# Summing passes of a four-layer graph network: key numbers read from PSUM, and twelve gather buffers in place of six

## The reference

```python
edge_index = jnp.stack([src, dst])
x = x + L0(h, edge_attr)          # sum of edge features by dst, then an MLP
x = x + L1(h, edge_attr)          # attention over the edges of a node
# L2: sums in both directions
agg_fwd = segment_sum(w[:, None] * x[col], row)
agg_bwd = segment_sum(w[:, None] * x[row], col)
out = 0.5 * (agg_fwd @ W_src.T + b_src) + 0.5 * (agg_bwd @ W_dst.T + b_dst)
# L3: weighted mean over src rows by dst, matmul, layernorm
ssum = segment_sum(edge_weight[:, None] * node[src], dst)
```

## Time and profile before

| | us |
|---|---|
| median of 3 runs | 9346.08 (9331.73 to 9353.26) |
| the profiled execution: its own time | 9342.07 |
| the profiled execution: span from first to last instruction | 9340.4 |
| forward L2 pass, first gather to last addition | 5389.4 to 6194.1 |
| backward L2 pass | 6896.4 to 7573.4 |
| L3 pass | 8432.1 to 9140.3 |
| mean granted TensorE clock | 0.881 |

### The profile page before, as it was taken

One profiled execution on the slowest core, in us unless ns is written; L12 is line 12 of the kernel. 1 busy time (PEld: TensorE's weight loads), 2 busy tenths in 40 slices (PEclk: granted clock), 3 DMA queues, 4 the chain that ended last, 5 costly groups with the idle time before them and its releaser, 6 DMA issues. The chain is left out here.

```text
span 9340.4 us, 229910 instructions
## 1 busy us (share of the span) xinstructions
PE 7261.6 (78%) x60542; PEld 5838.2 (63%) x60851; DVE 6413.4 (69%) x20871; ACT 3252.4 (35%) x9379; POOL 4037.3 (43%) x4385
## 2 busy tenths in 40 slices
PE   4855677899968888888868977758877775886777
PEld 4855566544446666666667766646666664666665
DVE  5999888511167777777777766656666676666667
ACT  3533322222223333333235500025520025557882
POOL 2000577000057777777625567730037740006771
PEclk7975789999977777777789999989999988999997
DMA  0000466300024444444347866665556644556663
GB/s 21 2 2 1 110 140 140 91 24 24 23 73 105 107 105 106 106 105 105 91 147 271 289 183 191 191 156 230 230 199 191 192 156 178 230 230 183 184 182 106
DMA packets 645062, 1262.07 MB, mean 135 GB/s; under 512 B 126526, under 2 KB 183433, under 8 KB 644569
## 3 DMA queue, kind: packets, MB, share of 16 engines
q1 hardware_dynamic: 424337, 704.50, 23.0%
q0 software_dynamic: 199040, 544.46, 21.7%
q10 hardware_dynamic: 21452, 10.20, 0.4%
HBM read 780.96 MB, written 477.75 MB: 135 GB/s over the span
## 5 line engine op out<-in xcount | busy, mean ns | idle before, releaser
L1063 PE MATMUL PS<-w,GS 128*128 128x128 f32 x12176 | 1641.7, 284 | 499.9 <-DVE AREA L1008 224.2
L1063 PEld LDWEIGHTS PS<-w,GS 128*128 128x128 f32 x12176 | 1459.6, 192 | 682.3 <-DVE w L967 437.6
L1188 POOL DMA_INDIRECT GS<-xbuf,KI x964 | 1031.2, 1070 | 1759.7 <-ACTq L132 710.1
L1171 POOL DMA_INDIRECT GS<-t1d,KI x1564 | 1493.6, 955 | 488.0 <-issue 459.6
L2395 DVE TENSOR_SCALAR AREA<-PS,IP 128x512 bf16<-128x512 f32 x1116 | 837.7, 751 | 439.6 <-PE PS L2405 361.1
L967 DVE TENSOR_TENSOR w<-IO,KI 128x512 f32<-128x512 f32 (+1 forms) x1355 | 808.6, 597 | 424.6 <-issue 413.4
L2419 PE MATMUL PS<-AREA 128*128 x13392 | 961.1, 220 | 11.1 <-ACT GS L2373 1.4
L2419 PEld LDWEIGHTS PS<-AREA 128*128 128x128 bf16 x13392 | 843.8, 98 | 170.2 <-issue 49.2
L2373 ACT ACTIVATE GS<-PS 128x512 f32<-128x512 f32 x1116 | 666.3, 597 | 613.8 <-PE PS L2419 613.5
L1188 POOL DMA_INDIRECT GS<-pbuf,XR x558 | 595.3, 1067 | 209.4 <-issue 101.4
L1598 ACT ACTIVATE w<-PS,w 128x48 f32<-128x48 f32 x1564 | 341.7, 301 | 926.9 <-PE PS L1593 926.9
(11 more groups left out here) (410 smaller groups left out, 12508.2 us busy)
## 6 DMA issues: line engine op xcount, KB each, us to landing
xbuf<-GS SPq DMA_DIRECT2D x1116, 256.0 KB
XR<-in_edge_attr SPq DMA_DIRECT2D x780, 256.0 KB
pbuf<-AREA SPq DMA_DIRECT2D x482, 256.0 KB
GS<-t1d,KI POOLq DMA_INDIRECT x1564
GS<-xbuf,KI POOLq DMA_INDIRECT x964
GS<-pbuf,XR POOLq DMA_INDIRECT x558
AREA<-t2d ACTq DMA_DIRECT2D x121, 64.0 KB
keyd<-AREA POOLq DMA_INDIRECT x482
```

Of the source, the lines that this page charges most:

```text
L1063: i = e.matmul(PS[:, s % 3, 0:128], feats(s)[0:m, r, 0:D], SELW[s % 3][0:m, width * r:width * r + 128], start=(r == 0), stop=(r == 3))
L1171: e.indirect_dma_start(GS[0:m, s, r, 0:wide], None, table, bass.IndirectOffsetOnAxis(ap=idx[0:m, c:c + 1].bitcast(U32), axis=0)).then_inc( ...
L1188: e.indirect_dma_start(GF[:, 512 * s:512 * s + 512], None, buf, bass.IndirectOffsetOnAxis(ap=idx[:, b:b + 1].bitcast(U32), axis=0)).then_i ...
```

## The change

Three edits, all in code that the three summing passes use:

- `sel` reads the numbers 0 to 127 from PSUM (bank 7, the first 128 columns), where one `tensor_copy` at the start of each pass puts them. The keys stay in SBUF. Layer 0 goes on reading `IO` from SBUF.
- Twelve gather buffers (`GRING`): six in `GS` as before, six in `R`, the last third of `AREA`. GpSimd waits for `bd` from the thirteenth batch on (`b - GRING + 3`).
- The loops of VectorE, TensorE and ScalarE in these passes unroll 12 batches (`un=GRING`) and go round half as often. The 12 bounds of 6 batches are still loaded with one load for each 6 batches, twice in a round now. 558 = 46 x 12 + 6 and 482 = 40 x 12 + 2, so 6 and 2 batches follow the loop, each with a load of its own (before: none and 2).

```diff
-    def batches(e, nb, step):
+    def batches(e, nb, step, un=UN):
...
-        n = nb // UN
+        n = nb // un
         with e.Fori(0, n) as it:
-            for s in range(UN):
-                step(it * UN + s, s, it, False)
+            for s in range(un):
+                step(it * un + s, s, it, False)
...
-    def unit_ranges(e, nb, part):
+    def unit_ranges(e, nb, part, un=UN):
...
-            if s == 0:
-                held[0] = ranges(e, part, it * (2 * UN), 2 * UN)
-            return held[0][2 * s:2 * s + 2]
+            if s % UN == 0:
+                held[0] = ranges(e, part, it * (2 * un) + 2 * s, 2 * UN)
+            return held[0][2 * (s % UN):2 * (s % UN) + 2]
...
+        num = PS[:, 7, 0:width] if not srel else IO[:, 0:width]
+
         def sel(e, s, kl):
-            return e.tensor_tensor(SEL[s % 3], IO[:, 0:width].unsqueeze(1).to_broadcast([128, 4, width]),
+            return e.tensor_tensor(SEL[s % 3], num.unsqueeze(1).to_broadcast([128, 4, width]),
                                    kl.unsqueeze(2).to_broadcast([128, 4, width]), ALU.is_equal)
...
+            if not srel:
+                e.tensor_copy(num, IO[:, 0:width])
...
+    GRING = 12
+
+    def gslot(s):
+
+        return GF[:, 512 * s:512 * s + 512] if s < 6 else R[:, 512 * (s - 6):512 * (s - 5)]
+
     def gather_groups(p, bd, buf, idx, nb):
...
             for b in range(nb):
-                s = b % UN
-                if b >= UN:
-                    e.wait_ge(bd, b - UN + 3)
-                e.indirect_dma_start(GF[:, 512 * s:512 * s + 512], None, buf,
+                s = b % GRING
+                if b >= GRING:
+                    e.wait_ge(bd, b - GRING + 3)
+                e.indirect_dma_start(gslot(s), None, buf,
...
-        edge_pass(p, nb, 128, 128, part, keys, lambda s: GF[:, 512 * s:512 * s + 512].rearrange("p (r f) -> p r f", r=4),
-                  ready, 16, ACC, weight=weight)
+        edge_pass(p, nb, 128, 128, part, keys, lambda s: gslot(s).rearrange("p (r f) -> p r f", r=4),
+                  ready, 16, ACC, weight=weight, un=GRING)
```

More of the change, by code:

```diff
@@ L925, in gnn @@
     NIT = NBF // UN
-    def batches(e, nb, step):
-        n = nb // UN
+    def batches(e, nb, step, un=UN):
+        n = nb // un
         with e.Fori(0, n) as it:
-            for s in range(UN):
-                step(it * UN + s, s, it, False)
-        for s in range(nb % UN):
-            step(n * UN + s, s, n, n * UN + s == nb - 1)
-    def unit_ranges(e, nb, part):
+            for s in range(un):
+                step(it * un + s, s, it, False)
+        for s in range(nb % un):
+            step(n * un + s, s, n, n * un + s == nb - 1)
+    def unit_ranges(e, nb, part, un=UN):
         held = {}
-        n = nb // UN
+        n = nb // un
         def get(b, s, it, last):
@@ L943, in get, with edge_pass @@
                 return ranges(e, part, 2 * b, 2)
-            if s == 0:
-                held[0] = ranges(e, part, it * (2 * UN), 2 * UN)
-            return held[0][2 * s:2 * s + 2]
+            if s % UN == 0:
+                held[0] = ranges(e, part, it * (2 * un) + 2 * s, 2 * UN)
+            return held[0][2 * (s % UN):2 * (s % UN) + 2]
         return get
-    def edge_pass(p, nb, tail, width, part, keys, feats, ready, rstep, ACC, weight=None, count=False, srel=False):
+    def edge_pass(p, nb, tail, width, part, keys, feats, ready, rstep, ACC, weight=None, count=False, srel=False, un=UN):
         acc, mmd, oh, bd, dv, kx = (p.sem(n) for n in ("acc", "mmd", "oh", "bd", "dv", "kx"))
@@ L988, in _ @@
             e.nop().then_inc(acc, 3)
-            get = unit_ranges(e, nb, part)
+            get = unit_ranges(e, nb, part, un)
             if count:
@@ L1038, in step @@
                     i.then_inc(sr, 1)
-            batches(e, nb, step)
+            batches(e, nb, step, un)
             for q, w_ in (((nb - 2) % 3, wq), ((nb - 1) % 3, wp)):
@@ L1176, in gather @@
         return ready
+    GRING = 12
+    def gslot(s):
+        return GF[:, 512 * s:512 * s + 512] if s < 6 else R[:, 512 * (s - 6):512 * (s - 5)]
     def gather_groups(p, bd, buf, idx, nb):
-        ready = [p.sem(f"g{s}") for s in range(UN)]
+        ready = [p.sem(f"g{s}") for s in range(GRING)]
         @p.on("gpsimd")
@@ L1184, in _ @@
             for b in range(nb):
-                s = b % UN
-                if b >= UN:
-                    e.wait_ge(bd, b - UN + 3)
-                e.indirect_dma_start(GF[:, 512 * s:512 * s + 512], None, buf,
+                s = b % GRING
+                if b >= GRING:
+                    e.wait_ge(bd, b - GRING + 3)
+                e.indirect_dma_start(gslot(s), None, buf,
                                      bass.IndirectOffsetOnAxis(ap=idx[:, b:b + 1].bitcast(U32), axis=0)
                                      ).then_inc(ready[s], 16)
-            for s in range(UN):
-                e.wait_ge(ready[s], 16 * ((nb - 1 - s) // UN + 1))
+            for s in range(min(GRING, nb)):
+                e.wait_ge(ready[s], 16 * ((nb - 1 - s) // GRING + 1))
         return ready
```

## The result

The changed kernel takes 9129.93 us (median of 4 runs, 9122.88 to 9136.56), the kernel before on the same chips 9343.43. The ratio is 0.9772, 95% interval 0.9755 to 0.9789: 213.5 us faster. The prediction was 9135 and 211 us less. The profiled execution has a span of 9131.8 us, 208.6 less than the 9340.4 of before.

What follows compares the result with a forecast made beforehand. GpSimd, issuing gathers, was taken to bound the summing passes. Savings of 68, 59 and 85 us make 212, less 1 for copies: 211 off the 9346.08 median, so 9135 us; 8-in-10 range 9110 to 9235.

Steps and rivals of the forecast that it cites:

- What bounds the kernel: Three summing passes: GpSimd saturated in both L2 passes, at busy time plus 0.30 us; in L3 also 0.05 waiting for buffers.
- (a) numbers in PSUM: Gathers of the summing passes go from 1.067 to 0.957 us, GpSimd's period to 1.26 us.
- (b) the followers: TensorE at 1.07, ScalarE at 1.25 in L3 and VectorE at 1.20 us per batch stay below GpSimd's 1.26.
- The floor: VectorE's shortest time per batch with twelve to a round: 1.16 to 1.24 us, taken as 1.20.
- The round of 7.43 us in the earlier trace: Early L3 round of six batches, gathers in store, 1.238 us each; used for VectorE's floor.
- (c) twelve buffers: GpSimd gets six gathers ahead at each pass's start, 7.6 us a pass; L3's extra 0.05 us per gather goes.
- (d) the end of forward L2: Last 61 gathers, bound by transfers: twelve buffers fill at most the missing 9%, period 1.65 to 1.55 us.
- (e) the leftover batches: Six batches behind forward L2's loop, each with its own load, cost 3 to 5 us, taken as 4.
- the copies: Copy of the numbers at the start of each pass: under 0.7 us, three times, taken as 1 us in all.
- the fetch rival: Doubled loop body leaves the instruction store: one fetch a round 9315 us (chance 0.03), two 9585 (0.05); together 0.08.
- The lower end of the range: Whole kernel at 9110 us, if transfers at the end of forward L2 no longer bound, 18 us.

Runs made afterwards that it cites:

- the run with PSUM alone: The changed kernel with numbers in PSUM but six buffers and six batches to a round: 9218.36 us against 9344.10 for the kernel before.
- the two runs with six: The changed kernel with six buffers, six batches to a round: 9218.36 us; and with twelve to a round but six buffers in use: 9210.90 us.
- the short body with eighteen: The changed kernel with eighteen buffers and batches to a round, VectorE's part for batches spanning over 128 nodes left out of the summing passes: 9122.80 us.
- the runs with twenty and forty instructions more: The changed kernel with twenty or forty one-element memsets on VectorE ahead of forward L2: 10858.36 and 10843.64 us, against 10660.97 for the kernel before.
- with 346: The changed kernel with twenty-four buffers and batches to a round, VectorE's part for wide batches left out in every second batch: 9132.03 us.
- 404 and 538: The changed kernel with eighteen buffers and batches to a round: 9393.74 us; with twenty-four: 9310.49 us.

## Why the prediction was right

The steps that make up most of the gain were right: what bounds the passes, what a gather costs with the numbers in PSUM, and what the buffers do in L3 and at the start. One step was wrong in its mechanism, the end of forward L2, and a rival was kept off by luck. That the total came within 3 us is partly luck too: the three passes gave back 205.2 us where 212 were forecast, and the intervals of the times are 16 us wide to either side.

- **What bounds the kernel:** right. Two readings carried it: GpSimd's pause of 0.30 us behind every gather, so that an engine busy 74% was full; and the collision seen in the timeline. Without gathers the L2 passes go at 1.11 us a batch, and GpSimd's 1.263 is 0.957 plus 0.305. This holds on the chips where the kernel before takes 9337 to 9344 us, not on the one where it takes 10,661.
- **(a) numbers in PSUM:** forecast 0.957 and 1.26, measured 0.958 and 1.263. Three doses (none, half, all of `sel` in SBUF) give 0.957, 1.01 to 1.02, 1.03 to 1.06 us. The accumulation, with one input in SBUF and one in PSUM, was the right row to take for the changed `sel`. By what the Trainium skill infers in "SBUF — State Buffer" ("Who interferes with whom"), that `tensor_tensor` doesn't stall descriptor generation, the run with PSUM alone would have stood at 9344; it stood at 9218, so the measurement decides against it. The Trainium skill's rule on two SBUF inputs, in the same section, fits: the gathers are held back only beside a `sel` with both inputs in SBUF.
- **(b) the followers:** the conclusion was right, the size off. The floor is 1.11 us, not 1.20, and outside the bounds given (1.16 to 1.24). The round of 7.43 us in the earlier trace rows was not as free as taken: its head idles 1.80 us where the heads without gathers idle 1.40, and one of its steps took 1.03 us beside others of 0.91. That cost nothing, as the floor is not the bound.
- **(c) twelve buffers:** right in L3 (1.373 without them, 1.263 with them) and at the start (pause 4.9 for 12.3). In the L2 passes six were already enough in the middle.
- **(d) the end of forward L2:** wrong, though its number was met. The forecast was that twelve buffers fill the missing 9% of the DMA share and so speed the transfers. The share did rise from 0.91 to 0.98, but the rate stayed at 157 GB/s. The 70/45 = 1.556 us a gather (forecast 1.55) is an average of gathers at 1.26, issued while buffers were still free, and of later ones at 1.72, no faster than the 1.68 to 1.74 of before. What GpSimd gained by issuing early came back in the drain, the time from the last gather's start to the last addition: 6135.1 - 6115.6 = 19.5 us, where the sum took 8.7 plus 4. That is why forward L2 gave back 60.8 us and not 68. The drain goes with the number of buffers in use: 9.5 and 9.9 us in the two runs with six, 19.5, 19.8 and 19.7 in three with twelve, 29.7 in the short body with eighteen. A gather's 256 KB at 157 GB/s are 1.67 us (an estimate), so a full ring of twelve is 20.
- **(e) the leftover batches:** the 4 us are not seen. With six buffers the drain is 9.5 us without batches behind the loop and 9.9 with six. Of the copies no run shows more than that they fit in the total.
- **The range and the rivals:** the fetch rival had its mechanism right and its size and its place wrong. A stall comes with five to seven fetches a round and costs 3 to 5 us, where one or two fetches at 2.0 to 2.3 us each were taken, and it is VectorE that stalls and not TensorE. That the changed kernel escaped it was luck: all three of its loops were on the good side, the profile of before could not tell, and with the same loop length one pass of three stalled in the runs with twenty and forty instructions more. The lower end of the range was meant as 9135 - 18, which is 9117 and not 9110.

What is open: the exact rule of the fetches. The Trainium skill, "Runtime: NRT & Kernel Launch", section "Instruction fetch mechanics", gives a window of two pages of 16 KB; the trace shows fetches of 8 KB for VectorE, and no loop of 136 instructions ever fetched. The rule tried here, at most three pages of 128 instructions, failed in the run with forty. It rests on my counts, which the fetches themselves contradict in size.

## What to carry to other kernels

An engine may be at its limit below 100% busy: here the limit was busy time plus a pause of 0.30 us behind each gather, so look at the smallest and largest pause before calling an engine idle. An indirect gather of GpSimd that started while a 128x512 `tensor_tensor` of VectorE with two inputs in SBUF was running was held back by it; putting the constant input in PSUM cost one copy a pass and took 0.1 us off the average gather. More buffers let an engine issue ahead, but where the transfers themselves are the limit the time comes back in the drain. After unrolling a loop further, look for instruction fetches in the DMA view: of loops of the same length one stalled and others did not, and the stall was 3 to 5 us a round. And measure on more than one chip before you call a gain general.

## What the runs showed of the hardware that I had not expected

- VectorE's longer loops fetch their code again each round, in blocks of 8 KB: none or 5, 6 or 7 per round, with a median idle head of 4.3 to 6.4 us instead of 1.4. By the count of the compiled list, with 270 instructions it happened in no pass of the changed kernel and in 1 of 3 in each of two runs on another chip; with 346 in 1 of 3; with 404 and 538 in all; with 117 and 136 never.
- A branch back of VectorE costs 0.39 us beside the load of 12 bounds (heads of 1.40 and 1.01 us without gathers).
- How long a `sel` holds a gather back depends on how the two streams lie to each other: gathers with the same instructions around them averaged 1.031 to 1.077 us.
- At the end of forward L2 the DMA share rose from 0.91 to 0.98 and the rate stayed at 157 GB/s.
- One program takes 9340 us on some chips and 10,661 on another, at mean granted clocks of 0.88 and 0.81.
